# Residual, centring and squares of a layer norm moved into the last graph convolution of a two-part graph network

## The reference

```python
def conv(h, W, b):
    m = jnp.concatenate([h[dst], h[src], edge_attr], axis=1) @ W + b
    return jax.ops.segment_sum(m, dst, num_segments=n_nodes)
h = jax.nn.relu(conv(x, W1, b1))
h = jax.nn.relu(conv(h, W2, b2))
return conv(h, W3, b3)
...
m = jnp.mean(x, axis=axis, keepdims=True)
v = jnp.var(x, axis=axis, keepdims=True)
return (x - m) / jnp.sqrt(v + eps)
...
x = _layernorm(x + _L0_gnn_ref(x, edge_attr_16, edge_index, ...), axis=-1)
x = _layernorm(x + _L1_gnn_ref(x, edge_index, edge_attr_16, ...), axis=-1)
```

## Time and profile before

| | us |
|---|---|
| three runs of the kernel | 8165.77, 8168.19, 8173.2 |
| median | 8168.19 |
| the profiled execution | 8174.99, its span 8173.2 |
| gathers of the third convolution | from 2608.80 to 3652.5 |
| first DMA of the first norm | 3691.42 |
| first DMA of the pass behind it | 3756.96 |
| PE busy over the whole span | 6802.5 (83%) |
| POOL busy over the whole span | 5625.7 (69%) |
| DVE busy over the whole span | 4408.9 (54%) |
| granted TensorE clock, mean of the span | 0.889 |

### The profile page before, as it was taken

How to read it: one execution, slowest core, us unless ns; L and a number is a source line. 1 busy time by engine, 2 the same in 40 slices (tenths; PEclk the granted TensorE clock), 3 DMA queues, 4 the chain that set the end, 5 groups by cost and what they waited for, 6 DMA issues and landing times. The chain is left out here.

```text
span 8173.2 us, 167770 instructions
## 1 busy us (share of the span) xinstructions
PE 6802.5 (83%) x53896; PEld 5558.7 (68%) x53897; DVE 4408.9 (54%) x5887; ACT 2345.3 (29%) x3848; POOL 5625.7 (69%) x5891
## 2 busy tenths in 40 slices
PE   5999999889897889885888888878768887888885
PEld 4777777788886888884566666666556666666663
DVE  7888886322222222225566566666556666665655
ACT  4878786100000000002222222222322222222223
POOL 4666664477775777765777777777467777777773
PEclk9999998788887888887898898999889889888987
DMA  5666666577776777773222222222222223222222
GB/s 182 237 240 241 236 244 194 181 266 283 276 281 229 278 280 282 260 241 117 69 70 67 71 74 66 70 72 67 56 77 72 71 67 75 67 72 67 71 69 63
DMA packets 415308, 1226.32 MB, mean 150 GB/s; under 512 B 120178, under 2 KB 219852, under 8 KB 366574
## 3 DMA queue, kind: packets, MB, share of 16 engines
q1 hardware_dynamic: 214343, 743.70, 25.4%
q0 software_dynamic: 187712, 233.42, 13.9%
q10 hardware_dynamic: 13160, 248.08, 7.5%
HBM read 943.22 MB, written 281.51 MB: 150 GB/s over the span
## 5 line engine op out<-in xcount | busy, mean ns | idle before, releaser
L1947 POOL DMA_INDIRECT data<-q_rows,idx x3328 | 3152.0, 947 | 1145.0 <-issue 1001.8
L922 POOL DMA_INDIRECT data<-h_parts,idx x2508 | 2427.2, 968 | 1204.6 <-issue 1020.5
L1054 PE MATMUL p_z<-hs,adj 128*128 128x192 bf16 x22442 | 2118.4, 252 | 61.2 <-issue 61.2
L1054 PEld LDWEIGHTS p_z<-hs,adj 128*128 128x128 bf16 x22442 | 1936.5, 100 | 313.6 <-issue 105.7
L2079 ACT COPY back<-p_back 128x1024 f32<-128x1024 f32 x418 | 423.0, 1012 | 2380.6 <-PE p_back L1967 2380.6
L2149 DVE TENSOR_TENSOR_SCAN run<-reset,run,p_turn 128x1024 f32<-128x1024 bf16 x416 | 974.4, 2342 | 146.0 <-PE p_turn L2014 140.4
L1169 ACT CAST adj<-p_count 128x1012 bf16<-128x1012 f32 x836 | 919.5, 1100 | 214.5 <-PE p_count L1040 191.8
L575 DVE TENSOR_TENSOR hot<-p_ramp,ends 128x2048 f32<-128x2048 f32 x416 | 949.9, 2284 | 0.6 <-issue 0.5
L1973 PE MATMUL part<-hot,t 128*128 128x128 f32 x6688 | 909.7, 295 | 45.5 <-issue 45.5
L1973 PEld LDWEIGHTS part<-hot,t 128*128 128x128 f32 x6688 | 880.0, 213 | 46.1 <-issue 46.1
L1978 PE MATMUL part<-hot,back 128*128 128x128 f32 x6688 | 815.3, 275 | 0.0
(11 more groups left out here) (327 smaller groups left out, 6386.8 us busy)
## 6 DMA issues: line engine op xcount, KB each, us to landing
adj<-counted SPq DMA_DIRECT2D x304, 1568.0 KB
counted<-adj ACTq DMA_DIRECT2D x76, 3136.0 KB
reset<-flags SPq DMA_DIRECT2D x208, 512.0 KB
data<-q_rows,idx POOLq DMA_INDIRECT x3328
data<-h_parts,idx POOLq DMA_INDIRECT x2508
feat<-in_ea_blocks SPq DMA_DIRECT2D x208, 128.0 KB
ea<-in_ea_cols SPq DMA_DIRECT2D x154, 88.0 KB
rden<-node_rows SPq DMA_DIRECT2D x50, 256.0 KB
```

The costliest lines, as they stand in the source:

```text
L922: pool.indirect_dma_start(out=data[:, p % HELD, j, 0:PARTS], out_offset=None, in_=table[:, :], in_offset=bass.IndirectOffsetOnAxis(ap=idx[ ...
L1054: mm = pe.matmul(p_z[:, 0:PARTS], adj[:, (q + LAG) % 2, hi, :], hs[:, hi, :], start=(hi == 0), stop=(hi == BLOCKS - 1))
L1947: pool.indirect_dma_start(out=data[:, r, j, :], out_offset=None, in_=q_rows[:, :], in_offset=bass.IndirectOffsetOnAxis(ap=idx[:, r, j:j + ...
```

## The change

The third convolution takes over the residual and half of the norm. DVE's `rows` for the last layer adds x to the sum, reduces over the 64 features, scales the sums to means, subtracts them, squares, and reduces the squares into `var`, all quad by quad (`normalised`). The rows stored are centred and go to `x1_rows` itself. SP loads the quad's x rows into `x_in` (one buffer) at the head of `store`, and after the last store writes the 100 sums of squares of each partition to `var_rows`.

The pass behind it becomes `first_rows`: it loads those sums and one set of 5 pieces instead of two; ACT takes one root of all sums, DVE inverts them once, DVE (not POOL) scales each piece, and DVE (not ACT) copies to `q_stage`. `w.source` is loaded by SP behind piece 0, and PE waits for it alone before its first multiplication; the other 16 shared loads are issued by POOL.

```diff
@@ conv_pass
+        if last:
+            x_in = sb("x_in", [P, QUAD, D])
+            squares = sb("squares", [P, QUAD, D])
+            means = sb("means", [P, 2, QUAD])
+            var = sb("var", [P, HB])
+            s_x = sem("s_x")
...
             def store(n):
+                if last:
+                    sp.dma_start(x_in[:, :, :], by_partition(x_rows)[:, bass.ds(n * QUAD, QUAD), :]).then_inc(s_x, 16)
                 sp.wait_ge(s_h, n + 1)
...
-            sp.wait_ge(s_out, 32 + 16 * QUADS)
+            if last:
+                sp.dma_start(var_rows, var[:, :]).then_inc(s_out, 16)
+            sp.wait_ge(s_out, 32 + 16 * QUADS + (16 if last else 0))
...
-                    to = out[:, bass.ds((n & 1) * QUAD, QUAD), :]
-                    v.wait_ge(s_step, n + 1)
-                    gate(v)
-                    v.tensor_tensor(to, conv[:, :, :], part_s[:, :, 0:D], ALU.add).then_inc(s_conv, 1)
-                    v.wait_ge(s_conv, n + 2)
-                    v.memset(scratch[:, 0:1], 0.0).then_inc(s_h, 1)
+                    normalised(n)
...
+            def normalised(n):
+
+                to = out[:, bass.ds((n & 1) * QUAD, QUAD), :]
+                step = lambda i: [v.wait_ge(s_step, n * 6 + i), gate(v)]
+                step(1)
+                v.tensor_tensor(conv[:, :, :], conv[:, :, :], part_s[:, :, 0:D], ALU.add).then_inc(s_conv, 1)
+                v.wait_ge(s_conv, n + 2)
+                v.wait_ge(s_x, n * 16 + 16)
+                gate(v)
+                v.tensor_tensor(to, conv[:, :, :], x_in[:, :, :], ALU.add).then_inc(s_step, 1)
+                step(2)
+                v.tensor_reduce(means[:, 0, :], to, AX_X, ALU.add).then_inc(s_step, 1)
+                step(3)
+                v.tensor_scalar(means[:, 1, :], means[:, 0, :], 1.0 / D, None, ALU.mult).then_inc(s_step, 1)
+                step(4)
+                v.tensor_tensor(to, to, means[:, 1, :].unsqueeze(2).broadcast_to([P, QUAD, D]), ALU.subtract)\
+                 .then_inc(s_step, 1)
+                step(5)
+                v.tensor_tensor(squares[:, :, :], to, to, ALU.mult).then_inc(s_step, 1)
+                step(6)
+                v.tensor_reduce(var[:, bass.ds(n * QUAD, QUAD)], squares[:, :, :], AX_X, ALU.add).then_inc(s_h, 1)
@@ first_norm becomes first_rows
+            sp.dma_start(var[:, 0, :], var_rows).then_inc(s_var, 16)
             for n in range(PIECES):
-                sp.dma_start(piece(b, n), view(b_rows, n)).then_inc(s_a[n], 16)
-                sp.dma_start(piece(a, n), view(a_rows, n)).then_inc(s_a[n], 16)
-            for tile, rows in shared:
-                sp.dma_start(tile, rows).then_inc(s_shared, 16)
+                sp.dma_start(b[:, piece(n), :], by_partition(x_rows)[:, piece(n), :]).then_inc(s_b[n], 16)
+                if n == 0:
+                    sp.dma_start(*shared[2]).then_inc(s_source, 16)
...
         def _(pool):
-            for n in range(PIECES):
-                norm.scale(pool, n)
+            rest = shared[:2] + shared[3:]
+            for tile, rows in rest:
+                pool.dma_start(tile, rows).then_inc(s_shared, 16)
+            pool.wait_ge(s_shared, 16 * len(rest))
...
+            nc.scalar.activation(var[:, 1, :], var[:, 0, :], ACT.Sqrt, bias=eps[:, 0:1], scale=1.0 / D).then_inc(s_sd, 1)
+            for c in range(NCH):
                 act.wait_ge(s_turn, c + 1)
                 if c >= 2:
                     act.wait_ge(s_q, c - 1)
                 nc.scalar.copy(x_t[:, c % 2, :], p_x[:, c % 2, 0:PAIR]).then_inc(s_xt, 1)
...
+            v.reciprocal(var[:, 2, :], var[:, 1, :]).then_inc(s_rsd, 1)
...
+            def scale(n):
+                v.wait_ge(s_b[n], 16)
+                by = var[:, 2, piece(n)].unsqueeze(2).broadcast_to([P, W, D])
+                v.tensor_tensor(b[:, piece(n), :], b[:, piece(n), :], by, ALU.mult).then_inc(s_norm, 1)
+
+            scale(0)
+            for c in range(NCH):
+                if c % CHUNKS == 0 and c // CHUNKS + 1 < PIECES:
+                    scale(c // CHUNKS + 1)
+                v.wait_ge(s_q, c + 1)
+                if c >= 2:
+                    v.wait_ge(s_q_out[c % 2], 16 * (c // 2))
+                v.tensor_copy(q_stage[:, c % 2, :, :], p_q[:, c % 2, 0:B * D].rearrange("p (b f) -> p b f", b=B))\
+                 .then_inc(s_stage, 1)
```

84 lines of the change are left out of this document (33 added, 51 removed).

## The result

The changed kernel takes **8182.68 us** (median of 20 runs, 8177.12 to 8189.02), the kernel before 8170.41 us in the same measurement (20 runs, 8165.63 to 8175.41). The ratio is 1.0014 with an interval of 1.0008 to 1.0021. The change costs 12 us in this measurement, where I had forecast a gain of 8, and the time lies outside my range.

The account below looks back on a forecast made before the run. POOL's gathers were taken to bound the third convolution, landings of q rows the pass behind from the third copy on. Tail +8.5 and pass -16.5 summed to -8 us: 8160 from the 8168.19 median, forecast 8153 to 8166, range 8149 to 8174.

Parts of the forecast that it names:

- In-turn cost 0: Third convolution: the added DVE steps, +3.5 us a quad, and x loads hide within the turns, costing 0.
- D: Rival: late s_nodes holds PE in two-quad turns, +12 us, 8172; chance 0.16 shared with the rival of a costlier tail.
- the sums of this shape don't slow the gathers: Third convolution: argument against DVE steps holding up POOL's gathers (8208 us); that or another loss over 0.2% had chance 0.08.
- Tail +8.5: Last four quads of the third convolution: +8.0 us by DVE steps and x loads, +0.5 for storing sums; bounds 5 to 11.
- First copy at T + 8.7: Pass behind, T its first DMA: first q rows copied at T + 8.7, 19.5 us earlier than before.
- Third copy at T + 15.2: Pass behind, T its first DMA: third copy waits for 5.65 MB of loads at 419 GB/s plus a store; 15.6 us earlier.
- bound of 13: Pass behind: lowest gain expected, with a backlog at half the rate and DVE late at each piece; upper bound 20.
- "1 us off" for ACT and 31.7 us from the third copy on: Pass behind: landings of q rows set the 31.7 us from third to last copy; 1 us less without ACT's squares.
- 16.5: Pass behind the third convolution: total gain in us, bounds 13 and 20.
- PNA 0: The two PNA passes, whose code the change doesn't touch: forecast difference 0 us.
- PE, DVE and ACT "together" are under half busy: Pass behind, before the change: reading of the profile page, with the DMA engines at 0.63.
- x is hidden at the first quad of a turn: Third convolution: x load issued behind the last half of a 1568 KB table lands in time, no cost.

Follow-up runs that it names:

- e12: After, with a wait at the end of POOL's part of first_rows repeated, adding five idle instructions: 8178.45 us.
- e15: After, with x rows loaded a quad ahead, five q_stage buffers and five idle POOL instructions: 8162.19 us, ratio to before 0.9980 to 0.9998.
- e7: Before, with five buffers for q_stage instead of two: 8165.15 us.
- e9: The new pass behind alone, after the third convolution of before: 8173.69 us.
- e11: After, with only x added per quad; mean, centring, squares and their sum left out: 8170.73 us.
- e14: Before, with eleven more idle POOL instructions at the end of its part of the first norm pass: 8171.34 us.
- e1: After, unchanged, measured and profiled once more: 8178.45 us.
- e3: After, with POOL's 16 table loads held back, one for each q chunk copied: 8180.99 us.
- e5: After, with h3_rows kept so the DRAM tensors stand at their addresses of before: 8178.83 us.
- e10: The new third convolution alone, ahead of the norm pass of before: 8179.61 us.
- e13: After, with 16 small memsets of an unread tile on POOL behind its table loads: 8180.91 us.
- e2: After, with x rows in two buffers, each loaded one quad ahead: 8175.78 us.
- e8: Before, with w.source loaded by SP behind the first piece and the 16 other tables issued by POOL: 8175.30 us.
- e18: After, with the 16 table loads back in SP's queue: 12708.31 us on a chip with a lower TensorE clock, where before took 12716.45.
- e4: After, with five buffers for q_stage instead of two: 8170.86 us.

## Why the prediction was wrong

Between the -8 us of the sum and the +6.3 of the profiled executions lie 14.3 us: 8.4 in the pass behind, 5.0 in the PNA passes, 2.7 in the gathers; the tail gives 1.6 back and the rest 0.2. Two steps failed, then: the term for the backlog ahead of the third copy, and the PNA passes, which the sum had at nothing without a reason.

- **In-turn cost 0:** right for the turns (no wait of PE or POOL grew by more than the spread of rows; D didn't happen), wrong for the gathers' own length: +2.7 us, by gathers that start while DVE reads two operands in SBUF. I had written that the sums of this shape don't slow the gathers and that no run shows it, from a mean of 944 ns. The trace of before does show it, in 2 gathers of 836 (that of 2954.62 took 1.17 us, that of 3455.53 1.00); only one sum a quad was of that kind, and the chain has more. How much it comes to hangs on where the steps fall between the gathers, which is luck: 1.4 us in e12 to 3.9 in e15, with the same steps, and 0.3 to 1.3 in before, e7 to e9, e11 and e14. This is the smaller error.
- **Tail +8.5:** right within 2 us: 6.9 to 7.9 in the eight profiles with this convolution (after, e1, e3 to e5, e10, e12, e13), with the waits for x in b and d as forecast, and one in c (2.35 us) that I had put at nearly nothing. By e2 it is half round trip and half DVE; by e11 the round trip shows only behind the chain.
- **First copy at T + 8.7:** 10.2. The sums and the root were as counted, and DVE begins its first scaling at T + 4.9 (forecast 4.7). But the first copy stands behind the second scaling in DVE's program, and that waits for its rows to 3709.57 and takes 1.49 us. I had put the scalings under the x1 stores and overlooked that one.
- **Third copy at T + 15.2:** this is the step of the pass that failed. It came at T + 22.6, 7.4 us late, and 5.3 to 5.8 late in the seven other profiles. The bytes were right, the rate and the ends were not: the windows give 0.48 MB by 3704 where 419 GB/s from T would give 1.3 (2.0 us), 267 GB/s in 3708 to 3712 (1.5 us), some 400 elsewhere (0.6 us); the other 3.3 us I put down to the landing of the q store itself, which the term left out; that split is worked out, not shown, though the DMA engines were done over 2 us ahead of the copy. e3, without the tables, is still 4.4 us later than the sum would have it. My bound of 13 for the pass's gain allowed 3.5 us for all that. What I had cited from the Trainium skill held ("DMA: Bandwidth & Descriptors", section "Issuing engines are not separate DMA queues"): the tables are in the way wherever they are issued (e8, e18), and held back they bring the copy forward (e3).
- **"1 us off" for ACT and 31.7 us from the third copy on:** measured 31.7, and 29.6 to 32.7 in the other profiles. The round trips set it, not ACT (e4, e7). And the two terms aren't independent: e3 brings the third copy to T + 13.9 and pays 6.2 us of it back behind it. Even a right backlog would not have given 16.5.
- **PNA 0:** this is the other step that failed: 5.0 us given back in the profile of after and 9.0 in the mean of ten, in code that the change doesn't touch; no part of my sum or of my rivals had it. e9 and e10 put it behind the new pass, e18 ties it to the table loads on POOL by one profile, and its cause stays open. In the profiles it turned a loss of 1.5 us (+2.7 + 6.9 - 8.1) into one of 6.3; the other 6 or so of the 12 are the distance of the two profiled executions from their medians. My range was made of the bounds of the two stretches that I had looked at.
- **Readings:** that PE, DVE and ACT "together" are under half busy in the first norm holds for each of them alone (25.2, 32.5 and 25.0 of 65.6 us). That x is hidden at the first quad of a turn was wrong, at no cost.

With the measured terms the sum is 8174.99 + 2.7 + 6.9 - 8.1 + 5.0 - 0.2 = 8181.3, against 8181.55 for the profiled execution of after; the 0.2 is the start of the convolution and the rest. That the terms add up shows only that no stage is missing.
